# The last attention head of a transformer layer: which units are split, which engine makes their low parts, and when the experts' tokens are placed

## The reference

```
xn  = layernorm(x)
q, k, v = xn @ Wq + bq, xn @ Wk + bk, xn @ Wv + bv          # 16 heads
s   = q @ k.T / sqrt(32) + alibi, masked causally
ctx = softmax(s) @ v;            attn = ctx @ Wo + bo
probs = softmax(norm_w * rmsnorm(xn) @ router_w.T);  two best experts e, weights w
y   = 4 * sum over the two of  w_e * (silu(xn @ gate_e) * (xn @ up_e)) @ down_e
out = x + attn + y
```

## Time and profile before

| | |
|---|---|
| times of 3 runs | 1922.46, 1926.85, 1927.61 us; median 1926.85 |
| the profiled execution | 1924.57 us, span from first to last instruction 1922.8 us |
| busy in the span | PE 1870.5 us (97%), DVE 1506.5, ACT 1415.9, POOL 1406.0 |
| mean granted clock of TensorE | 0.990 |

### The profile page before, as it was taken

How to read it: one execution, slowest core, us unless ns; L and a number is a source line. 1 busy time by engine, 2 the same in 40 slices (tenths; PEclk the granted TensorE clock), 3 DMA queues, 4 the chain that set the end, 5 groups by cost and what they waited for, 6 DMA issues and landing times. The chain is left out here.

```text
span 1922.8 us, 39426 instructions
## 1 busy us (share of the span) xinstructions
PE 1870.5 (97%) x8656; PEld 1441.3 (75%) x8657; DVE 1506.5 (78%) x3497; ACT 1415.9 (74%) x2790; POOL 1406.0 (73%) x1214
## 2 busy tenths in 40 slices
PE   6999999999999999999999999999998989999997
PEld 5788777777777777777777777777756767888875
DVE  6454466898999989999999998999957956666664
ACT  4333322999999999999999999999972235555554
POOL 5111113899999999999999999999948846666665
PEclk9999999999999999999999999999999999999998
DMA  8577767542423424234242342423217756556553
GB/s 274 199 245 257 270 221 235 143 106 63 107 74 77 106 63 110 71 78 104 63 111 70 79 103 63 119 63 83 77 41 230 251 178 122 103 104 108 104 98 65
DMA packets 119242, 242.14 MB, mean 126 GB/s; under 512 B 17632, under 2 KB 54368, under 8 KB 112896
## 3 DMA queue, kind: packets, MB, share of 16 engines
q1 hardware_dynamic: 101120, 205.84, 36.7%
q0 software_dynamic: 18080, 35.81, 10.2%
HBM read 139.28 MB, written 104.21 MB: 127 GB/s over the span
## 5 line engine op out<-in xcount | busy, mean ns | idle before, releaser
L1175 POOL TENSOR_TENSOR probs_lo<-probs,probs_hi 128x512 fp32r<-128x512 f32 x812 | 1020.2, 1300 | 79.4 <-ACT probs L1210 76.4
L1209 ACT ACTIVATE probs_hi<-s_ps 128x512 fp32r<-128x512 f32 x967 | 680.9, 704 | 26.1 <-DVE s_ps L1282 22.2
L1210 ACT ACTIVATE probs<-s_ps 128x512 f32<-128x512 f32 x933 | 637.5, 702 | 10.2 <-DVE s_ps L1282 6.6
L1261 DVE TENSOR_REDUCE m_part<-m_ps 128x1 f32<-128x512 f32 x744 | 477.8, 682 | 3.0
L1518 PE MATMUL s_ps<-q_st,k_st 100*128 100x512 f32 (+3 forms) x880 | 310.5, 385 | 1.1 <-DMA q_st<-m_rows 0.8
L1502 PE MATMUL m_ps<-k_st,q_st 98*128 98x512 f32 (+2 forms) x840 | 291.1, 382 | 1.3 <-DVE v_raw L776 0.8
L1537 PE MATMUL o_ps<-probs_hi,v_split 128*96 128x512 f32 (+3 forms) x741 | 272.4, 375 | 1.7 <-POOL probs_lo L1175 1.7
L1538 PE MATMUL o_ps<-probs_lo,v_split 128*96 128x512 f32 (+3 forms) x741 | 273.8, 371 | 0.0
L1258 DVE CUSTOM_DVE_ANT_0 m_ps<-m_ps,mask_row 128x128 f32<-128x128 f32 x496 | 244.4, 493 | 16.4 <-PE m_ps L1502 7.8
L1518 PEld LDWEIGHTS s_ps<-q_st,k_st 100*128 100x128 f32 x880 | 162.9, 190 | 61.3 <-ACT probs L1210 22.0
L623 POOL TENSOR_TENSOR v_rows<-v_raw,v_rows 128x512 fp32r<-128x512 f32 x32 | 41.3, 1294 | 228.9 <-ACT v_rows L679 228.9
(11 more groups left out here) (236 smaller groups left out, 3728.3 us busy)
## 6 DMA issues: line engine op xcount, KB each, us to landing
v_d<-v_rows SPq DMA_DIRECT2D x7, 3072.0 KB, 9.4
v_split<-v_d SPq DMA_DIRECT2D x22, 768.0 KB, 8.3
k_st<-k_hi_d SPq DMA_DIRECT2D x44, 256.0 KB
q_st<-q_hi_d SPq DMA_DIRECT2D x44, 256.0 KB
xn_d<-xs SPq DMA_DIRECT2D x8, 1024.0 KB, 11.8
q_hi_d<-qk_hi SPq DMA_DIRECT2D x32, 256.0 KB, 7.7
q_lo_d<-qk_lo SPq DMA_DIRECT2D x32, 256.0 KB, 7.8
k_hi_d<-qk_hi SPq DMA_DIRECT2D x32, 256.0 KB, 3.5
```

Source lines behind the costliest of these rows:

```text
L1175: nc.gpsimd.tensor_tensor(*low_operands(u), ALU.subtract).then_inc(lo_ready_pool, 1)
L1209: nc.scalar.activation(probs_hi[:, P_SLOT[u]], scores, ACT.Exp, scale=SCALE)
L1210: nc.scalar.activation(scores if kind == "Q" else probs[:, P_SLOT[u]], scores, ACT.Exp, scale=SCALE).then_inc(p_ready, 1)
L1261: V.tensor_reduce(top, scores, AX.X, ALU.max).then_inc(m_taken, 1)
```

## The change

In the last head, units 0 to 14 and 17, 20, 23, 26, 29, 32 are whole, 21 of 34 (before: all but 21, 23, 25, 27, 29, 30, that is 28). The other 13 are of kind Q, their low parts by VectorE, each put behind the next unit's scores in the list. Wo's low part goes from GpSimd to VectorE, at unit 22. GpSimd has then no work of its own in the last head. The placing of the tokens begins at unit 1 instead of 3 and takes two to three steps at each unit (one at unit 4) instead of one, two and later three; the count goes ahead of unit 6 (before: 9), the exponential for it behind unit 1 (before: 6), the spread matrix to unit 1 (before: 5). The inverses of the first batch go from unit 4 to unit 16, and SP's part of them from behind the stores of head 30's fourth chunk to behind those of head 31's second chunk, with the loads of gate and up weights that stand behind it. The high part of Wo goes to units 3 to 6 (before: 11, 13, 15, 17).

```diff
-LAST_WHOLE = [u for u in range(NS) if u not in (21, 23, 25, 27, 29, 30)]
+LAST_WHOLE = (*range(15), 17, 20, 23, 26, 29, 32)
-LAST_KIND = "".join("PW"[u in LAST_WHOLE] for u in range(NS))
+LAST_KIND = "".join("QW"[u in LAST_WHOLE] for u in range(NS))
 # last_order
             order.append(("S", u, 0))
+        if 0 < u <= NS and LAST_KIND[u - 1] == "Q":
+            order.append(("D", u - 1, 0))
 # SP, attention
-                    if (kind, u, back) == ("O", QCS - 1, 1):
+                    if (kind, u, back) == (("O", QCS - 1, 1) if maxima else ("O", 1, 0)):
 # GpSimd
-                    if is_last(n) and (kind, u) == ("S", 24):
-                        split_wo()
 # ScalarE
-                    if is_last(n) and kind == "S" and u == 6:
+                    if is_last(n) and kind == "S" and u == 1:
                         share_weights()
-                    if is_last(n) and kind == "S" and 10 <= u < 10 + 2 * G and u % 2:
-                        high_wo((u - 10) // 2)
+                    if is_last(n) and kind == "S" and 3 <= u < 3 + G:
+                        high_wo(u - 3)
 # VectorE
-                        for _ in range((u >= 3) + (u >= 8) + (u >= 13)):
+                        for _ in range((u > 0) + (u > 0 and u != 4) + (u > 0 and not s_diagonals(u) and u != 4)):
                             next(pieces, None)
-                        if u == 4:
+                        if u == 16:
                             first_inverses()
-                        if u == 5:
+                        if u == 22:
+                            dve.wait_ge(wo_hi_ready, G)
+                            V.tensor_tensor(t["wo_lo"], t["wo_raw"], t["wo_hi"].bitcast(F32), ALU.subtract).then_inc(wo_lo_ready, 1)
+                        if u == 1:
                             spread_matrix()
 # TensorE
-                    if not maxima and (kind, u) == ("S", 9):
+                    if not maxima and (kind, u) == ("S", 6):
                         count_tokens()
```

More of the change, by code:

```diff
@@ L1180, in step_n @@
                         low_part(n - back, u)
-                    if is_last(n) and (kind, u) == ("S", 24):
-                        split_wo()
-            def split_wo():
-                pool.wait_ge(wo_hi_ready, G)
-                nc.gpsimd.tensor_tensor(t["wo_lo"], t["wo_raw"], t["wo_hi"].bitcast(F32), ALU.subtract).then_inc(wo_lo_ready, 1)
             step_n(0, before=False)
```

## The result

The changed kernel takes 1975.70 us (median of 4 runs, 1974.85 to 1977.01), the kernel before 1925.66 (4 runs, 1922.46 to 1927.61): 1.0262 times, 95% interval 1.0249 to 1.0274. Forecast were 1922.7, in 1917.0 to 1927.5. The profiled execution spans 1972.8 us (before 1922.8). In the changed kernel's numbering the scatters are L1706, the output's products L1831, the last take L1770.

The account below looks back on a forecast made before the run. TensorE bounds output stage and experts; GpSimd's late scatters cost it the gap between. Gap 5.4 us less, head 1.3 more: 4.1 less, 1922.7 us from the median 1926.85; range 1917.0 to 1927.5.

Parts of the forecast that it names:

- the last sentence on the head: Output stage after the last head: begins behind the same last add and stores, so only shifts with it; 0 us.
- Rival (3): Scatters beside a busy VectorE are slow, 2.28 us each, so token lists come later than before; 1944.7 us, chance 0.05.
- The gap ahead of the experts: Between output stage and experts: earlier token lists end TensorE's wait for xg; 5.4 us less, bounds 4.4 and 6.0.
- The first part: Last take to first transposes: transposes start at VectorE's take's end, 1554.05 instead of 1558.53; 4.5 us less.
- The second: First transposes to the second ones: the shorter gap keeps TensorE's clock up; forecast -0.9 us.
- The placing: Last head, placing of the tokens on the engines ahead of GpSimd's scatters: done at 1419.0.
- The head: Last head, to the output's first product: ends 1.3 us later in all, bounds 1.95 earlier and 4.0 later.
- Unit 18's stand: Last head: TensorE stands some 3 us before unit 18's scores, until unit 15's low part is done on VectorE.

Follow-up runs that it names:

- drain8: Changed kernel, GpSimd waiting after every 8 scatters until they have landed; 1925.72 us (0.9999 of the kernel before).
- pace32: Changed kernel with a GpSimd subtraction of 32 columns, read by nobody, behind each scatter; 1924.25 us.
- best: Changed kernel, 32-column subtractions behind the first 24 scatters, Wo's low part back on GpSimd, first inverses at unit 18; 1920.70 us (0.9975 of the kernel before).
- plain: Changed kernel with 64 plain GpSimd transfers where the scatters were, the scatters held until the first context columns' low part is made; 1948.88 us.
- hold: Changed kernel with all 64 scatters held until VectorE has made the low part of the first context columns; 1931.87 us (1.0030 of the kernel before).
- twice: Changed kernel with the 64 scatters issued twice in one train, the second time into a scratch table; 2050.69 us.
- pacelate: Changed kernel with GpSimd's 32-column subtraction behind scatters only from the 21st on; 1933.55 us.
- dvepause: Changed kernel with ten more VectorE subtractions of two SBUF operands in units 24 to 33 of the last head; 1974.56 us.
- paced24: Changed kernel with GpSimd's 32-column subtraction behind the first 24 scatters only; 1923.16 us (0.9988 of the kernel before).

## Why the prediction was wrong

- **The step that failed** is the last sentence on the head: the output stage "begins behind the same last add and stores, so it shifts with it". It was costed at nothing and came to +51.89 us. I had read from the earlier trace rows that nothing that leaves other engines there changes that stage, and looked at what GpSimd's scatters do to their own pace only. In runs without the stall the sentence holds: 108.21 (drain8), 108.81 (pace32), 108.71 (best) against 108.36. The exception is plain, whose columns came late (114.87).
- **What decided instead.** In the kernel before, scatters run at 1.27 us too, but only from 1441 to 1451; then VectorE's adds of the output stage lengthen about every second one, and the mean of the earlier trace rows is 1.65. GpSimd's timeline of the kernel before, where this begins (VectorE subtracts two SBUF operands from 1451.37 to 1452.59):

```profile
1448.92 0.97 POOL L1707 DMA_INDIRECT list_d<-pairs,slot  x1 [0.31 <-issue]
1450.19 0.96 POOL L1707 DMA_INDIRECT list_d<-pairs,slot  x1 [0.30 <-issue]
1451.46 1.97 POOL L1707 DMA_INDIRECT list_d<-pairs,slot  x1 [0.30 <-issue]
1453.73 0.97 POOL L1707 DMA_INDIRECT list_d<-pairs,slot  x1 [0.31 <-issue]
```

  I took the 1.65 as the scatter's own pitch. Started at 1420.8, where VectorE works mostly on PSUM, the train keeps 1.27 for 25 us up to the step into the output stage, but for one scatter of 2.27 us beside Wo's low part. From 1468 on it holds itself up: as VectorE gets no work, it lengthens no scatter. That the train does it is shown (hold, pace32, twice). That its pitch decides is the reading that fits pace32, pacelate and the kernel before; that the train is unbroken because VectorE is idle is read from the traces, and the run for it (dvepause) did not decide.
- **Rival (3)** had the scatters as the culprit with the opposite sign: slow beside a busy VectorE. The slowest did take 2.27 us, but the mean pitch was 1.31, not 2.28, and the harm was that they were quick.
- **The gap ahead of the experts** was right in its cause; that its size came out (-5.64 and +0.45 make -5.2, forecast -5.4) is partly luck. The first part was 1.1 us better, because VectorE's counter rises as the last take starts and not at its end. The second was 1.35 worse: the first products ran at full clock, and then TensorE waited 1.70 us for the next rows.
- **The placing** ended at 1420.52, forecast 1419.0; the first scatter 1.6 us late. That cost nothing.
- **The head** came 1.1 us later than forecast (+2.37 for +1.3). Unit 18's stand was 2.52 us for 3. VectorE's two insertions, the inverses at unit 16 and Wo's low part, cost some 2.5 us: paced24 and best, which differ in them, have medians 2.46 apart (head's end, in one execution each, 1448.36 and 1445.32). Which wait of the head was mis-sized is open.
- **The sum without the failed step**: forecast -4.1 us, paced24 against before -2.36 (1923.16 - 1925.52), best -4.82.

## What to carry to other kernels

A row of indirect transfers on GpSimd is not free for the others: when moving one, ask what sets its pitch where it will stand, and look for "issue" waits on engines that have nothing to do with it. A wait of several engines at once, without a semaphore, in equal steps, points to something that the engines share and not to the code in which they stand. Cheap work between the transfers (0.26 us here) was enough to keep the stall away, and one pause of 1.41 us among them was not.

## What the runs showed of the hardware

- Indirect scatters of 128 pairs, issued by GpSimd one per 1.27 us, brought TensorE and SyncE to steps of 0.70 us or a multiple for each instruction, and VectorE and ScalarE stood with TensorE as it began; at 1.56 us, with a subtraction between two, they did not, and plain transfers at 0.54 us did not. What they share is open.
- The stall is no late block of TensorE's instructions, as far as the rows go. The Trainium skill's page Runtime: NRT & Kernel Launch (Instruction fetch mechanics) says that a sequencer fetches its next block of instructions by a queue of its own while it runs the current one, so that it is mostly hidden. In the changed kernel one transfer of an instruction queue falls into 1482 to 1483, with 245 weight loads and products of TensorE since the one before (1418.3 to 1482.3); before the change there were 254 between two of them (1417.3 to 1456.3). So the block came when as much had been used up, in the midst of the stall:

```profile
q8 instruction: 1, 0.02, 5.8%
```

- A scatter that starts while VectorE subtracts two SBUF operands took 1.97 us in place of 0.97 (the kernel before, 1451.46). One that started 0.1 us ahead of such a subtraction took 0.97 (the changed kernel, 1443.91). That this is part of why the kernel before does not stall is a reading; no run here decides it.
